# A mixture-of-experts stage with full and half tiles in place of 39 full ones

## What is computed

```python
x = x + cross_attention(layernorm(x), ctx_1024, ...)
xf = layernorm(x).reshape(-1, 128)
scores = sigmoid(xf @ gate_w + bias)
top_scores, top_idx = top_k(scores, 2)          # then normed, w: [T, E]
up = einsum('th,ehi->tei', xf, up_w) + up_b     # 128 -> 512, 8 experts
hact = gelu(up)
eo = einsum('tei,eih->teh', hact, down_w) + down_b
combined = einsum('teh,te->th', eo * 0.1, w)
shared = (gelu(xf @ sw_up + sb_up) @ sw_down + sb_down) * 0.1
out = shared + combined
x = x + out / (max(abs(out), axis=-1) + 1e-6)
```

## Times and profile before

| | us |
|---|---|
| median of 3 runs | 894.63 (893.97 to 895.32) |
| the profiled execution, its own time | 891.31 |
| its span, first to last instruction | 889.6 |
| PE busy in the span | 808.4 |
| DVE busy | 644.3 |
| ACT busy | 652.1 |
| POOL busy | 555.5 |

### The profile page before, as it was taken

One profiled execution on the slowest core, in us unless ns is written; L12 is line 12 of the kernel. 1 busy time (PEld: TensorE's weight loads), 2 busy tenths in 40 slices (PEclk: granted clock), 3 DMA queues, 4 the chain that ended last, 5 costly groups with the idle time before them and its releaser, 6 DMA issues.

```text
span 889.6 us, 21772 instructions
## 1 busy us (share of the span) xinstructions
PE 808.4 (91%) x7005; PEld 548.2 (62%) x7005; DVE 644.3 (72%) x1767; ACT 652.1 (73%) x1185; POOL 555.5 (62%) x647
## 2 busy tenths in 40 slices
PE   5899999989999999999877649999999999999994
PEld 2355555545555555554555437888888888888673
DVE  5656677788687787767575356877877778777797
ACT  3478887867877877876796539988888888889530
POOL 7456665878878787877565723156566665657531
PEclk9899999989999999999997869999999999999997
DMA  4442643441212222211001124567676788891983
GB/s 121 163 148 78 201 130 109 133 145 59 79 56 80 71 61 83 79 49 49 26 30 50 55 85 169 215 232 266 241 258 245 250 279 269 305 291 47 248 232 106
DMA packets 101383, 128.84 MB, mean 145 GB/s; under 512 B 21144, under 2 KB 81368, under 8 KB 95256
## 3 DMA queue, kind: packets, MB, share of 16 engines
q1 hardware_dynamic: 92183, 108.04, 37.9%
q0 software_dynamic: 9088, 19.42, 6.2%
HBM read 78.79 MB, written 40.56 MB: 134 GB/s over the span
## 4 chain that ended last, share of the span: by engine, by line
PE 62%; DVE 9%; issue 9%; POOL 8%; ACT 7%; another core or an unknown queue 3%; SPq 1%; DMA 0%; ACTq 0%; DVEq 0%; POOLq 0%
PE bank L1298 9%; PE bank L1283 6%; POOL y_scratch L1164 5%; ACT prob L734 5%; PE bank L1380 4%; PE bank L1378 4%; PE bank L1379 4%; PE bank L1389 4%; PE bank L1391 4%; PE bank L1390 4%; PE bank L1303 3%; PE bank L1315 3%; PE bank L1276 3%; PE bank L1258 2%
## 5 line engine op out<-in xcount | busy, mean ns | idle before, releaser
L734 ACT ACTIVATE prob<-bank,padb,sc 120x512 f32<-120x512 f32 x256 | 178.1, 776 | 75.5 <-PE bank L1303 69.8
L1164 POOL DMA_INDIRECT y_scratch<-yo,ti x156 | 156.3, 1002 | 121.8 <-DVE yo L1067 85.2
L1142 POOL TENSOR_SCALAR_AFFINE_SELECT prob<-prob 120x512 f32<-120x512 f32 x256 | 161.5, 634 | 84.0 <-ACT prob L734 78.4
L804 DVE TENSOR_REDUCE nm<-bank 128x4 f32<-128x480 f32 x256 | 150.4, 650 | 67.0 <-PE bank L1283 66.9
L1046 DVE TENSOR_TENSOR gl<-gf,gh 128x512 fp32r<-128x512 f32 x220 | 152.7, 696 | 55.8 <-ACT gh L780 50.4
L1157 POOL DMA_INDIRECT xs_scratch<-x2r,idx x128 | 126.2, 986 | 50.7 <-issue 33.0
L780 ACT ACTIVATE gh<-gf 128x512 fp32r<-128x512 f32 x220 | 138.5, 630 | 5.1
L1298 PE MATMUL bank<-qblk,kT 32*120 32x512 f32 x512 | 114.3, 649 | 0.1
L775 ACT ACTIVATE gf<-bank,wt 128x512 f32<-128x512 f32 x156 | 105.7, 678 | 0.3
L775 ACT ACTIVATE gf<-bank,shb 128x512 f32<-128x512 f32 x64 | 43.6, 681 | 47.8 <-remote 20.8
L1315 PE MATMUL bank<-prob,vm 120*32 120x128 f32 x2048 | 72.0, 281 | 1.2 <-issue 0.6
(11 more groups left out here) (194 smaller groups left out, 1658.8 us busy)
## 6 DMA issues: line engine op xcount, KB each, us to landing
wt<-w_scratch SPq DMA_DIRECT2D x39, 1032.0 KB
xt<-xs_scratch SPq DMA_DIRECT2D x39, 280.0 KB
w_scratch<-x2t SPq DMA_DIRECT2D x8, 1024.0 KB, 5.2
wt<-y_scratch SPq DMA_DIRECT2D x28, 256.0 KB, 4.8
xs_scratch<-padc SPq DMA_DIRECT2D x15, 280.0 KB, 3.8
x<-in_x SPq DMA_DIRECT2D x16, 256.0 KB, 3.1
qblk<-qT SPq DMA_DIRECT2D x64, 64.0 KB
x_scratch<-x SPq DMA_DIRECT2D x16, 256.0 KB, 2.4
```

The source lines that it names most:

```text
L734: e.activation(prob[u % NP][0:LK, :], banks[bi][0:LK, :], ACT.Exp, scale=sc[0:LK, 0:1], bias=padb[0:LK, t:t + 1]).then_inc(a_ex, 1)
L804: e.tensor_reduce(nm[:, g, i // 2, :], bk[:, 0:480].rearrange("p (j k) -> p j k", j=4), AX.X, ALU.max, negate=True).then_inc(v_mx, 1)
L1142: e.affine_select(out=pv, in_=pv, compare_op=ALU.is_ge, fill=0.0, base=0, pattern=[[0, 4], [1, 128]], channel_multiplier=-1).then_inc(p_cu ...
L1164: e.indirect_dma_start(y_dram, bass.IndirectOffsetOnAxis(ap=ti_[r % NWS][:, c:c + 1], axis=0), yo_[r % NYO][:, c, :], None).then_inc(d_y[r ...
```

## The change

32 full tiles and 7 half tiles of 256 rows take the place of 39 full ones. They come in a fixed pattern: four full tiles, then a half tile, seven times, and four full tiles at the end. For a half tile everything that goes by rows is halved: the load of the rows, 2 transposes in and 2 out, the columns of the up products, gelu, `gh`, `gl`, `xl`, `ye`, `yo`, and 2 scatters. Its down products still run over all 512 columns (the second half of `gh` and `gl` holds what an earlier tile left there, and nothing reads its result). Its weights are loaded in full.

```diff
-NT = 2 * TOK // T + NE - 1
+NFULL = 2 * TOK // T
+NHALF = NE - 1
+NT = NFULL + NHALF
+ROOMS = [q for h in range(NE) for q in [(h * NFULL // NE + j, False) for j in range(NFULL // NE)] + ([(h, True)] if h < NHALF else [])]
...
+PARTS = [GB // 2 if kind == "routed" and ROOMS[r][1] else GB for kind, r in TILES]
...
-        return end + TILE_FROM[EARLY] + 1.6 * (x - 4 * EARLY)
+        ti = min(int(x // 4), len(TILES))
+        rows = sum(PARTS[EARLY:ti]) + (x / 4 - ti) * (PARTS[ti] if ti < len(TILES) else GB)
+        return end + TILE_FROM[EARLY] + 1.6 * rows
...
-                    for c in range(4):
+                    for c in range(PARTS[n]):
                         ins = e.transpose(bk[:, 128 * c:128 * c + 128], xt_[r % NXT][:, c, 0:128], ident)
...
-                    bk = take(stage, n, i)
+                    bk = take(stage, n, i)[:, 0:LQ * PARTS[n]]
...
-                    xh, xl = xh_[n % 2][:, :], xl_[n % 2][:, :]
-                    e.matmul(bk[:, :], w[:, 128 * i:128 * i + 128], xh, start=True, stop=False)
+                    xh, xl = xh_[n % 2][:, 0:LQ * PARTS[n]], xl_[n % 2][:, 0:LQ * PARTS[n]]
+                    e.matmul(bk, w[:, 128 * i:128 * i + 128], xh, start=True, stop=False)
...
                     h, l = gh_[k % RG][:, :], gl_[k % RG][:, :]
```

The table must now say which expert's full tiles and which expert's half tile go where, with 17 entries (8 of full tiles, 8 of half ones, one end) in place of 9. It is also built so that full tiles that find no full place are cut over two half places. The constants that it reads make `con` wider (506 columns for 408), and its large steps use `kblk` and `qblk`, so that it waits for the last product with them (`m_B`):

```diff
-                    e.wait_ge(m_Q, NG)
-                    e.wait_ge(m_V, NG)
+                    e.wait_ge(m_B, 4 * NB)
...
+                    e.tensor_scalar(ctj[:, NE:2 * NE], cti[:, :], 8, 1, ALU.logical_shift_right, ALU.bitwise_and).then_inc(v_bar, 1)
...
+                    e.tensor_scalar(over[:, :], cB[:, 2 * NE - 1:2 * NE], float(NFULL), float(NFULL), ALU.max, ALU.subtract).then_inc(v_bar, 1)
...
+                    e.tensor_tensor(ge[:, :, :], tau[:, :].unsqueeze(2).to_broadcast([1, NT, NV + 1]),
+                                    cum[:, :].unsqueeze(1).to_broadcast([1, NT, NV + 1]), ALU.is_ge).then_inc(v_bar, 1)
```

More of the change, by code:

```diff
@@ L104, in constants @@
     c[:, C_BASE:C_BASE + 8] = REGION * np.arange(8) - 1
-    c[:, C_TAU:C_TAU + NT] = np.arange(NT)
-    c[:, C_EO:C_EO + 9] = 128 * np.minimum(np.arange(9), 7)
-    c[:, C_REG:C_REG + 9] = REGION * np.arange(9)
+    c[:, C_TAU:C_TAU + NT] = [NFULL + q // 2 if half else q for q, half in ROOMS]
+    c[:, C_TAV:C_TAV + NT] = [NFULL + q if half else 0 for q, half in ROOMS]
+    c[:, C_SUB:C_SUB + NT] = [q / 2 if half and q % 2 else 1e6 for q, half in ROOMS]
+    c[:, C_EO:C_EO + NV] = 128 * np.append(np.tile(np.arange(NE), 2), NE - 1)
+    c[:, C_REG:C_REG + NV] = REGION * np.append(np.tile(np.arange(NE), 2), NE)
     c[:, C_TOK:C_TOK + NB] = p[:, None] + LQ * np.arange(NB)
@@ L389, in xattn_moe_kernel @@
         cti = sb("cti", [1, NE], I32)
-        ctj = sb("ctj", [1, NE], I32)
-        cA = sb("cA", [1, 4 + NE])
-        cB = sb("cB", [1, 4 + NE])
-        cum = sb("cum", [1, NE + 2])
-        val = sb("val", [1, NE + 1])
-        ge = xhat[0:1, :, :].rearrange("p b d -> p (b d)")[:, 0:NT * (NE + 2)].rearrange("p (t e) -> p t e", t=NT)
-        ohe = xT[0:1, 0:NT * (NE + 1)].rearrange("p (t e) -> p t e", t=NT)
-        pre = cx_[0][0:1, 0:NT * (NE + 1)].rearrange("p (t e) -> p t e", t=NT)
+        ctj = sb("ctj", [1, 2 * NE], I32)
+        cA, cB, cC = [sb(name, [1, 3 * NE]) for name in ("cA", "cB", "cC")]
+        cum = sb("cum", [1, NV + 1])
+        val = sb("val", [1, NV])
+        over = sb("over", [1, 1])
+        tau = sb("tau", [1, NT])
+        sub = sb("sub", [1, NT])
         rowf = sb("rowf", [1, NT])
@@ new lines, in _ @@
+                    e.wait_ge(v_bar, 8)
+                    e.tensor_tensor(cum[:, 1:NV], cB[:, NE:3 * NE], cB[:, 0:2 * NE], ALU.add).then_inc(v_bar, 1)
+                    e.tensor_scalar(over[:, :], cB[:, 2 * NE - 1:2 * NE], float(NFULL), float(NFULL), ALU.max, ALU.subtract).then_inc(v_bar, 1)
+                    e.wait_ge(v_bar, 10)
+                    e.scalar_tensor_tensor(out=tau[:, :], in0=con[0:1, C_TAV:C_TAV + NT], scalar=over[:, :], in1=con[0:1, C_TAU:C_TAU + NT],
+                                           op0=ALU.subtract, op1=ALU.max).then_inc(v_bar, 1)
@@ new lines, in _ @@
+                    e.tensor_scalar(sub[:, :], con[0:1, C_SUB:C_SUB + NT], over[:, :], float(T // 2), ALU.is_lt, ALU.mult).then_inc(v_bar, 1)
+                    e.scalar_tensor_tensor(out=val[:, :], in0=cum[:, 0:NV], scalar=float(-T), in1=con[0:1, C_REG:C_REG + NV],
+                                           op0=ALU.mult, op1=ALU.add).then_inc(v_bar, 1)
+                    e.wait_ge(v_bar, 13)
+                    e.tensor_tensor(ge[:, :, :], tau[:, :].unsqueeze(2).to_broadcast([1, NT, NV + 1]),
+                                    cum[:, :].unsqueeze(1).to_broadcast([1, NT, NV + 1]), ALU.is_ge).then_inc(v_bar, 1)
@@ new lines, in _ @@
+                    e.scalar_tensor_tensor(out=val[:, NE:2 * NE], in0=cA[:, NE:2 * NE], scalar=float(T), in1=val[:, NE:2 * NE],
+                                           op0=ALU.mult, op1=ALU.add).then_inc(v_bar, 1)
+                    e.scalar_tensor_tensor(out=sub[:, :], in0=tau[:, :], scalar=float(T), in1=sub[:, :], op0=ALU.mult,
+                                           op1=ALU.add).then_inc(v_bar, 1)
+                    e.wait_ge(v_bar, 16)
+                    e.tensor_tensor(ohe[:, :, :], ge[:, :, 0:NV], ge[:, :, 1:NV + 1], ALU.subtract).then_inc(v_bar, 1)
@@ L1017, in _ @@
                     kind, r = TILES[n]
-                    src = banks[bank_of["t_xT", n, 0][0][0]][:, :] if kind == "routed" else x2t[:, r, :]
+                    w = LQ * PARTS[n]
+                    src = banks[bank_of["t_xT", n, 0][0][0]][:, 0:w] if kind == "routed" else x2t[:, r, :]
                     e.wait_ge(a_xh, n + 1)
```

121 lines of the change are left out of this document (65 added, 56 removed).

## The result

The changed kernel takes **927.8 us** (927.2 to 931.4, 4 runs); the kernel before took 895.0 (894.0 to 896.2, 4 runs) beside it on the same chip. The ratio is 1.039, with an interval of 1.035 to 1.043 (the two medians alone give 1.037). The forecast was 887.1, faster by 0.8%; it is slower by 3.9%.

A forecast was written before the change was run, and what follows sets the result against it. PE was taken to bound all routed tiles. From the profiled 891.3 us, -12.0 (narrow work) + 2.8 (table) + 1.5 (clock) + 0.2 (wider load) = -7.5 gave 883.8; with 3.3 carried over for the median, 887.1, range 884.0 to 891.0.

The forecast's parts named there:

- Part 1: Half tiles on PE: narrow matmuls at 0.125 us (or 0.116) and fewer transposes save 12.0 us (or 12.8).
- first rival: Half tiles on PE: a narrow matmul costs up to 0.231, as a wide one; 896.0 in full, chance 0.07 with others.
- Part 2: Beside a half tile PE stays the bound; ACT, POOL and weight loads were taken to cost 0.
- part 4: Behind PE's wait after the table: one stretch at 1.2 GHz, costing 1.5 us, bounds 0 and 3.0.
- Part 3: The longer table on DVE ahead of the routed tiles adds 2.8 us, all of it PE waiting, 3.2 us in total.
- short kind of stretch: Behind the table: a stretch of 3.2 us at the lower clock, costing 1.5 us; the longer kind is 6.6 us.
- bound of 3.0: Behind the table: the upper bound in us for the lower clock's cost, from the longer stretch of 6.6 us.
- third rival: At half tiles: late weights make PE wait and the clock fall, 3.7 us each for three; chance 0.06 with other losses.
- The clock falls there: At half tiles: a lower clock there was named as one sign that the prediction is wrong.

The follow-up runs named there:

- v1: The changed kernel with the table cut in four, small selects around the sends at half tiles and one behind every four hand-over scatters; 0.996 of the kernel before.
- x2: The changed kernel with the up products of a half tile at 512 columns again; 1.003 of the kernel before.
- x3: The changed kernel with POOL waiting, ahead of each piece it sends, for an up product that would be done anyway; 1.004 of the kernel before.
- w4: The kernel before with two small selects behind every four scatters of the last four portions of the hand-over; 0.991 of the kernel before.
- y1: The changed kernel with the sends of a half tile and of the full tile ahead of it some 2 us later; 0.996 of the kernel before.
- y2: y1 with the table also cut into four pieces placed at later points on DVE; 0.994 of the kernel before.
- z3: y2 with those sends waiting until the sends of the tile before have landed, in place of the up product; 1.017 of the kernel before.
- w1: y2 with those sends waiting for down product 4n+8 in place of the up product; 1.006 of the kernel before.
- z1: The kernel before with no work added; at seven routed tiles four sends are held back until the next four are ready; 1.088 of the kernel before.
- w2: y2 with the full tile ahead of a half tile waiting for up product 4n+12, the half tile for 4n+11; 1.002 of the kernel before.
- w3: The kernel before with two small selects behind the four sends of 35 routed tiles, inside the pause; 1.006 of the kernel before.
- z2: z1 with only the last two of the four sends held back; 1.070 of the kernel before.

## Why the prediction was wrong

**Part 1 was right**, at the lower of its two values: 0.115 per narrow matmul, 12.8 us in the sum. The first rival, a narrow matmul that costs as much as a wide one, is excluded. By the formula on the page "TensorE: Matmul & The Clock Gate" of the Trainium skill, section "Back-to-back issue gap", which the page calls that of an isolated matmul, these matmuls would take 109 ns; the rows have 115, and for 512 columns 231 against 216.

**Part 2 failed**, in one sentence: "POOL still sends four pieces for the full tile ahead and has 3 buffers of slack". Both halves are true and the conclusion, a cost of nothing, was false. Four sends are 4 x 1.26 = 5.04 us and the window is 5.1 (5.2 in the prediction, which worked it out for PE and ACT and did not set the sends beside it), since an engine that isn't the bound and has buffers to spare was taken to cost nothing. The price was not POOL's time. It was that two rows of sends became one, and PE's signals were late in it: 27.9 us of waits, and 12.3 more at the lower clock behind them. In the kernel before nothing of this shows in the routed tiles, but it showed in the hand-over, where POOL scatters without a pause and PE has waits of 4.00 and 15.8 us; part 4 used the first for the clock behind it and didn't ask what it waited for.

The rest of part 2 holds: ACT did not become the bound, and no PE wait between 560 and 825 us is for a DMA in any trace here, in v1 neither, where the windows are as short and nothing else is in the way.

**Part 3 was right in mechanism and nearly in size.** The table takes 7.87 us (7.74 forecast; the earlier trace rows), DVE first and then PE in order of time:

```profile
528.31 0.15 DVE L1008 TENSOR_TENSOR cnt<-run,con 1x8 f32<-1x8 f32 x1
...
530.53 0.88 DVE L1032 TENSOR_TENSOR kblk<-tau,cum 1x702 f32<-1x702 f32 x1
...
536.18 0.68 DVE L1088 TENSOR_TENSOR gl<-gf,gh 128x512 fp32r<-128x512 f32 x1
```

```profile
532.54 0.40 PE L1426 MATMUL bank<-xh,wsh 128*128 128x512 f32 x1
537.00 0.76 PE L1436 MATMUL bank<-gh,wsh 128*128 128x512 f32 x1 [4.06 <-DVE gl L1088]
```

PE waits 4.06 us for 3.2 forecast: the table began 1.26 us later than before while PE's last ready matmul ended 0.49 later, which is 0.77 of the 0.86.

**Part 4** named the right place and took the short kind of stretch; it was the long one, 6.7 us at 0.50. PE works for only 5.30 of them, so it cost 5.30 x 0.46 = 2.4 us for 1.5. (The bound of 3.0 took a stretch of 6.6 us to be all work; in the earlier trace rows PE is busy for 4.66 of it.) Together that is 3.7 + 2.4 = 6.1 us for 4.3; the first routed chunk was 5.4 late.

**The third rival** had the right picture, a PE wait and the lower clock at each half tile, and the wrong cause, weights, so it was priced at 3.7 us for three tiles and given 0.06 with others. Measured were 4.4 us of waits (4.05 and 0.35) and 1.6 to 2.4 by the clock at each of six, and one wait of 1.3 at the seventh. "The clock falls there", as what would prove the prediction wrong, is what happened. The clock was a consequence: without the waits (x2, x3, v1) it stays at 1.00 in the stage.

## What to carry over

Before a change shortens a window, lay the row of every engine beside it, those that have time to spare as well, and ask what stands in its pauses: a pause can be doing work that no busy share shows. On this kernel, keep indirect DMAs on GpSimd in rows of at most four, with a pause behind each and no signal of PE's due late in one. Small compute instructions break a longer row (w4, v1); a wait does so too (y1, y2), as long as it doesn't push the sends against the next row (z3, w1). And when half a kernel's gain is missing, look for the same cause where the kernel before already pays for it. When an engine starts long after what releases it has ended, look at who else was busy in between, not only at the releaser, and at the recorded times of the semaphore updates.

## What the runs showed of the hardware

- PE's semaphore updates come late in a row of GpSimd's indirect DMAs 0.30 us apart. Up chunks due 3.8 us (z1) and 4.3 us into a row (the kernel before) were seen on time; those due 4.1 (w2), 5.3 (the changed kernel) and 6.1 us into it (z1) were late, and so was a down product due 3.4 us into it (w2). What sets the limit is open.
- Single updates still come inside the row. The rest come in a burst behind it: the waiting engine goes on 1.0 (w2, a row of 4), 1.5 (the changed kernel, 8) and 1.4 us (z1, 12) after the row's end, and 3.6 us after a row of 24 (the kernel before). The burst of the changed kernel is seven updates, 604.19 to 604.50, 0.05 us apart.
- It is the update that is recorded late, and only PE's: 27 of 60 in the hand-over of the kernel before, none of ACT's or DVE's in any of the twenty traces. By which path the row holds them is open.
- A pause of 1.57 us ends it (2 of 321 updates late in the kernel before); 0.85 us with two small selects nearly does (w3, 30 of 276); rows broken by selects in v1 leave 0 of 405.
- The page "DMA: Bandwidth & Descriptors" of the Trainium skill, section "SWDGE vs HWDGE vs iDMA", tells of another coupling, in which DVE locks GpSimd out of the memory that it writes as it makes descriptors. The sends of the row of eight in the changed kernel start 1.26 to 1.46 us apart, as those of the rows of four in the kernel before do (1.26 to 1.40), so it isn't what is seen here.
- The hold feeds itself: a stall makes the next sends due before the row has ended, so that rows of eight and six became twelve and ten (z1, z2).
